# Four staging slots instead of two between the eviction and the store of relation products

## The reference

```
h = relu(layernorm(x))
# layer 0: a relational convolution, then a feed-forward part
xW  = einsum('nd,rde->nre', h, W_rel)        # 8 products per node
agg = segment_sum(xW[src, edge_type], dst)
y   = h + gelu(layernorm(agg + h @ W_self + b_conv))
x   = x + y + mlp(layernorm(y))
# layer 1: graph attention with 4 heads
xt = relu(layernorm(x)) @ W.T + bias
x  = x + segment_sum(xt[src] * softmax_over_dst(leaky_relu(...)), dst)
```

## Time and profile before

| | |
|---|---|
| median of three runs | 4581.68 us |
| profiled execution | 4576.85 us, its span 4575.1 us |
| busy share of PE, DVE, ACT, POOL | 55%, 55%, 13%, 70% |
| table stage: first store issued, last store issued | 21.77 us, 233.24 us |
| last store of the table stage landed | 235.86 us |
| stores of relation products | 98, of 512 KB each |
| gathers | 1680 from `rel_table`, 1664 from `xt_table` |

### The profile page before, as it was taken

How to read it: one execution, slowest core, us unless ns; L and a number is a source line. 1 busy time by engine, 2 the same in 40 slices (tenths; PEclk the granted TensorE clock), 3 DMA queues, 4 the chain that set the end, 5 groups by cost and what they waited for, 6 DMA issues and landing times.

```text
span 4575.1 us, 52415 instructions
## 1 busy us (share of the span) xinstructions
PE 2508.6 (55%) x13797; PEld 2111.2 (46%) x13902; DVE 2517.4 (55%) x6723; ACT 603.1 (13%) x1535; POOL 3194.7 (70%) x3372
## 2 busy tenths in 40 slices
PE   7923444444444444444433666666666666666664
PEld 3423343334434334443423556555555655555553
DVE  5652333333333333333334777777777777777777
ACT  4500111111111111111111000000000000000000
POOL 1077777777777777777746777777777777777772
PEclk9966676667667666766766777777777777877776
DMA  7722222222222222222213222222222222222222
GB/s 255 270 61 53 57 62 57 60 59 57 62 57 62 57 59 59 57 62 57 62 37 102 54 54 54 54 54 54 54 54 54 54 54 54 54 54 54 54 54 76
DMA packets 169389, 311.28 MB, mean 68 GB/s; under 512 B 58788, under 2 KB 99148, under 8 KB 168655
## 3 DMA queue, kind: packets, MB, share of 16 engines
q0 software_dynamic: 107008, 222.77, 20.2%
q1 hardware_dynamic: 46850, 81.19, 4.9%
q10 hardware_dynamic: 15490, 6.87, 0.6%
HBM read 239.51 MB, written 71.09 MB: 68 GB/s over the span
## 4 chain that ended last, share of the span: by engine, by line
POOL 66%; issue 23%; DVE 4%; DMA 3%; PE 2%; ACT 1%; POOLq 0%; DVEq 0%; ACTq 0%; SPq 0%
POOL G L490 66%; DMA rel_table<-G 2%; DMA G<-xt_table,idx 1%; DVE G L857 0%; DVE w L1223 0%; PE bank L1378 0%; PE bank L1379 0%; DVE G L1352 0%; DVE x_res L1354 0%; PE quad L1378 0%; PE quad L1379 0%; DVE edge L1226 0%; PE bank L1420 0%; ACT agg L724 0%; PE quad L1449 0%
## 5 line engine op out<-in xcount | busy, mean ns | idle before, releaser
L490 POOL DMA_INDIRECT G<-rel_table,idx x1680 | 1603.2, 954 | 743.6 <-issue 511.4
L490 POOL DMA_INDIRECT G<-xt_table,idx x1664 | 1570.7, 944 | 543.1 <-issue 502.3
L986 DVE SCALAR_TENSOR_TENSOR agg<-bank,sel,agg 128x128 f32 x208 | 64.2, 349 | 1057.0 <-PE bank L1420 1054.4
L1537 PEld LDWEIGHTS quad<-ident,top 128*128 128x128 f32 x3328 | 576.5, 272 | 143.8 <-issue 141.3
L1537 PE MATMUL quad<-ident,top 128*128 128x128 f32 x3328 | 585.1, 358 | 68.3 <-DVEq L1191 68.2
L1565 PE MATMUL bank<-M,onehot 128*128 128x132 f32 x3328 | 443.9, 289 | 172.5 <-DVE M L1240 172.5
L1565 PEld LDWEIGHTS bank<-M,onehot 128*128 128x128 f32 x3328 | 409.6, 198 | 204.5 <-issue 204.5
L1420 PE MATMUL bank<-G,onehot 128*128 128x128 f32 x1664 | 267.6, 336 | 391.2 <-DMA G<-rel_table,idx 386.8
L1420 PEld LDWEIGHTS bank<-G,onehot 128*128 128x128 f32 x1664 | 263.6, 253 | 395.8 <-issue 395.8
L1553 PE MATMUL bank<-Z,w_all 128*128 128x8 f32 x832 | 173.0, 337 | 442.7 <-issue 436.8
L1553 PEld LDWEIGHTS bank<-Z,w_all 128*128 128x128 f32 x832 | 166.2, 297 | 460.0 <-issue 459.8
(11 more groups left out here) (314 smaller groups left out, 3381.8 us busy)
## 6 DMA issues: line engine op xcount, KB each, us to landing
rel_table<-G SPq DMA_DIRECT2D x98, 512.0 KB, 2.7
G<-rel_table,idx POOLq DMA_INDIRECT x1680, 2.5
G<-xt_table,idx POOLq DMA_INDIRECT x1664, 2.7
xt_table<-w_all SPq DMA_DIRECT2D x25, 264.0 KB, 3.3
x_mid<-X SPq DMA_DIRECT2D x25, 256.0 KB, 2.0
out<-x_res SPq DMA_DIRECT2D x13, 448.0 KB
x_res<-in_x ACTq DMA_DIRECT2D x12, 448.0 KB, 4.4
x_res<-x_mid SPq DMA_DIRECT2D x3, 1792.0 KB, 10.5
```

Source lines behind the costliest of these rows:

```text
L490: g.indirect_dma_start(out=G[:, s, c, 0:width], out_offset=None, in_=table, in_offset=bass.IndirectOffsetOnAxis(ap=idx[:, s, c:c + 1], axi ...
L986: c.beside(v.scalar_tensor_tensor(row, banks[5 + k][:, 0:D], sel[:, w, bass.ds(g, 1)], row, ALU.mult, ALU.add))
L1537: ins = t.matmul(banks[j][:, hd * P:(hd + 1) * P], top[:, j, hd:hd + 1].to_broadcast([P, P]), ident[:, :], start=False, stop=(hd == HEADS ...
```

## The change

`STORES = 4` slots take the place of two. Block b uses slot b % 4, and each slot has its own semaphore `s_store[k]`, with a start value of 16 as before. ACT and DVE wait in block b for the store of block b-4. SP's loop runs 24 times over four blocks, and blocks 96 and 97 follow outside the loop; at the end SP waits for four semaphores. `hs`, `hT` and `typ_flat` move up by 2048 columns inside `G`. `hs`, `hT` and the two PSUM buffers of the products stay double.

```
+STORES = 4
+STORE_W = STORES * R * D
-        typ_flat = g_flat[0:GROUPS, 2 * R * D + 4 * D:2 * R * D + 4 * D + GROUP]
+        typ_flat = g_flat[0:GROUPS, STORE_W + 4 * D:STORE_W + 4 * D + GROUP]
-        xw = g_flat[:, 0:2 * R * D].rearrange("p (s n) -> p s n", s=2)
+        xw = g_flat[:, 0:STORE_W].rearrange("p (s n) -> p s n", s=STORES)
...
-        s_store = [sem("s_store0"), sem("s_store1")]
+        s_store = [sem(f"s_store{k}") for k in range(STORES)]
...
+            def store_block(b, k):
+                sp.wait_ge(xwA_sb, b + 3)
+                sp.wait_ge(xwB_sb, b + 3)
+                sp.dma_start(rel_table.rearrange("(n r) e -> n (r e)", r=R)[bass.ds(b * P, P), :],
+                             xw[:, k, :]).then_inc(s_store[k], 16)
+            with sp.Fori(0, BLOCKS // STORES) as i:
+                for k in range(STORES):
+                    store_block(i * STORES + k, k)
+            for b in range(BLOCKS // STORES * STORES, BLOCKS):
+                store_block(b, b % STORES)
+            for k in range(STORES):
+                sp.wait_ge(s_store[k], 16 * len(range(k, BLOCKS, STORES)) + 16)
...
-            def evict_high(b, j, pair):
+            def evict_high(b, j):
-                act.wait_ge(s_store[s], pair * 16 + 16)
-                a.copy(xw[:, s, 512:R * D], banks[2 + 3 * s][:, :]).then_inc(xwB_sb, 1)
+                act.wait_ge(s_store[b % STORES], b // STORES * 16 + 16)
+                a.copy(xw[:, b % STORES, 512:R * D], banks[2 + 3 * s][:, :]).then_inc(xwB_sb, 1)
...
-            def evict_low(b, s, pair):
+            def evict_low(b, s):
-                dve.wait_ge(s_store[s], pair * 16 + 16)
-                v.tensor_copy(xw[:, s, 0:512], banks[1 + 3 * s][:, :]).then_inc(xwA_sb, 1)
+                dve.wait_ge(s_store[b % STORES], b // STORES * 16 + 16)
+                v.tensor_copy(xw[:, b % STORES, 0:512], banks[1 + 3 * s][:, :]).then_inc(xwA_sb, 1)
```

More of the change, by code:

```diff
@@ L258, in build @@
         turn = s_flat[:, 5 * D + 24:5 * D + 24 + GROUPS].bitcast(i32)
-        xw = g_flat[:, 0:2 * R * D].rearrange("p (s n) -> p s n", s=2)
-        hs = g_flat[:, 2 * R * D:2 * R * D + 2 * D].rearrange("p (s n) -> p s n", s=2)
-        hT = g_flat[:, 2 * R * D + 2 * D:2 * R * D + 4 * D].rearrange("p (s n) -> p s n", s=2)
+        xw = g_flat[:, 0:STORE_W].rearrange("p (s n) -> p s n", s=STORES)
+        hs = g_flat[:, STORE_W:STORE_W + 2 * D].rearrange("p (s n) -> p s n", s=2)
+        hT = g_flat[:, STORE_W + 2 * D:STORE_W + 4 * D].rearrange("p (s n) -> p s n", s=2)
         hid = w_all[:, 0:2 * H].rearrange("p (s n) -> p s n", s=2)
@@ L394, in _ @@
                 sp.dma_start(tile[GROUPS - 1:GROUPS, 0:LAST], arr[full:E].rearrange("(g e) -> g e", g=1)).then_inc(s_edges, 16)
-            for k in range(2):
+            for k in range(STORES):
                 sp.sem_inc(s_store[k], 16)
[L398 to L406, removed]
+            def store_block(b, k):
[8 more added lines that the diff above has]
+                store_block(b, b % STORES)
+            for k in range(STORES):
+                sp.wait_ge(s_store[k], 16 * len(range(k, BLOCKS, STORES)) + 16)
             sp.sem_inc(tables_ready[0], 1)
@@ L617, in _ @@
                         act.wait_ge(h_norm, i + 2)
-                    evict_high(i * WIDE + j, j, i * (WIDE // 2) + j // 2)
+                    evict_high(i * WIDE + j, j)
                     load_ahead(i, j)
@@ L863, in low_round @@
                     more_stats(i, j)
-                evict_low(i * WIDE + j, j % 2, i * (WIDE // 2) + j // 2)
+                evict_low(i * WIDE + j, j % 2)
             turned(0, 0, [])
```

## The result

The changed kernel takes 4557.94 us (median of 5 runs, 4556.66 to 4560.1) against 4581.45 (4579.72 to 4583.63): ratio 0.995, 95% interval 0.9939 to 0.9962. In two later comparisons the gain at the medians was 22.5 and about 23 us. Between the first two profiled executions it is 19.3 us: 4575.1 to 4555.8 us of span.

A forecast was written before the change was run, and what follows sets the result against it. Waits for store slots were taken to bound the table stage, whose last store sets the kernel's end. Gains of rounds 0 to 6 summed to 16.85, say 17.0 us: 4581.68 - 17.0 = 4564.7 us, range 4559 to 4573.

The forecast's parts named there:

- The bound: Table stage, rounds 1 to 4: ACT and DVE wait for store slots; with four slots PE sets the pace.
- Loads of x: Table stage: two slots have 0.2 us of slack, and a load of x beside a store uses it up.
- Round by round, with round 5 as the measure of a round in which slots don't hold PE: Table stage: round 5's 26.15 us taken as PE's pace; rounds 2 and 3 fall to 26.2 us.
- rival B: Round 0: DVE gets its short steps in between two POOL instructions, 7.6 us more gain, 4557 us; chance 0.04.
- Round 1: Table stage: with weights W1, W2 and the linear weights besides, 30.80 to 27.2 us, gain 3.6.
- Round 0: Start of table stage: DVE still waits out POOL's block, block 6 copied at about 39.6; gain 0.7 us, bounds 0 and 2.5.
- The 84 rows: End of round 4: DVE waits 1.09 us for the last rows of x, PE's second buffer covers about half; 0.5 us stays.
- The change touches no gather: Behind the table stage: nothing in those 4340 us gets shorter; the kernel's end moves as much as the stage's last store.
- SP's two blocks outside the loop issue as in the loop: SP's blocks 96 and 97: no difference in issue; the new semaphores and increments cost under 0.1 us.
- A: Rival, table stage: DMA engines become the bound, not packed closer than 0.81; gain 8 us in all, 4574 us; chance 0.11.
- C: Rival, table stage: no change, stores wait behind each other whatever the slots; 4581.7 us; chance 0.06.
- D: Rival, round 0 onward: PE idles about 6.5 us and TensorE's low clock lasts; through round 1, 20 us slower, 4602; chance 0.03.

The follow-up runs named there:

- first experiment: Changed kernel with its four slots, but ACT and DVE wait for the store of block b-2 as before; 4577.84 us against 4578.69 for the kernel before.
- first try without loads of x: Kernel before, two slots, loads of x for rounds 3 to 6 left out and filled by POOL with a constant; 4571.53 us against 4578.69.

## Why the prediction was right or wrong

- **The bound** was right: the slot waits set rounds 1 to 4, they went, and PE took their place. Only the distance of the wait did it (first experiment).
- **Loads of x** as what uses up two slots' slack: right for 11.8 of 17.2 us, incomplete. Weight loads of 64 KB do it as well (rounds 1 and 2 of the first try without loads of x took 28.1 and 28.7 us), and with two slots a round without any other transfer still costs 0.8 us.
- **"Round by round, with round 5 as the measure of a round in which slots don't hold PE"** is the step that failed. A round that PE sets takes 25.8 us. The prediction had 14 x 1.83 = 25.6 for it, and read the 26.15 of round 5 as the same thing; but round 5 still held 0.8 us of slot cost around ACT's filling of `agg`: 2.27 and 2.38 us for two blocks, 1.83 and 2.01 in the changed kernel. Half of that was hidden, since the first seven blocks of the round took 12.5 us where the pace is 12.9: behind a stall the next blocks come faster. In the changed kernel the stall is the wait for the 84 rows; it shortens round 5 from 25.8 to 25.1 us, as the load moved earlier shows. With two slots it isn't shown that this wait is the reason: without other traffic rounds took 26.5 to 26.8 us, but in the first try without loads, which has no such wait, round 5 took 26.2 too.
- **The terms.** Term by term, forecast and measured gain, by the intervals between stores: round 1: 3.6, 5.0; round 2: 5.0, 5.4; round 3: 3.7, 4.1; round 4: 3.2, 2.6; round 5: 0.15, 1.1; round 6: 0.5, 1.1; round 0: 0.7, 0.8. With 0.3 us in the first store the sum is 20.4 at the last store, for 17. By the means of the three and four profiles the rounds 0 to 6 gained 1.1, 5.1, 4.8, 4.4, 2.6, 1.1 and 1.1 us. Round 6 was costed with 0.3 us for ACT's filling of `agg`, and four slots show none of it (2.17 us for that block, 2.14 for the others).
- **What that step explains.** The time is 6.8 us below the forecast's 4564.7. The rounds are 3.4 us of it. With 20.4 in the sum the forecast would have been 4561.3, inside the range; that the time fell below it comes with the 3.1 us by which the medians differ more than these last stores, see the last point. That it fell next to rival B's 4557 is chance, since B's way was not taken.
- **Round 1** at 27.2 for its weights: wrong by 1.4 us, the largest term. DMA share 0.99, PE without a gap. The estimate took a full DMA for a stall; with four slots, stores of that round took up to 5.2 us to land and nobody waited.
- **Round 0** was right by its mechanism. In the line numbers of before, I expected 776 to wait for line 466, 777 for 468 and 778 for the rest; in fact 777 got through as well, between 466 and 468, and 778 and 779 waited. The end, 39.6, is the same. The rule of the Trainium skill, page "SBUF — State Buffer", section "Who interferes with whom", agrees with this for the first two waits: 1.27 us behind line 474 and 4.37 behind 476 for 0.17 us of work, and 0.17 with POOL out of the way. The 3.11 us of the last step go further than the rule, which speaks of one instruction: they spanned four of POOL's, one close behind the other.
- **The 84 rows**: 1.65 us of wait instead of 1.09, and an interval of 3.3 us at the end of round 4 (before: the earlier trace rows):

```profile
159.06 0.68 DVE L780 BATCH_NORM_STATS2 stats<-x_res 128x6 f32<-128x128 f32 x3 [1.65 <-DMA x_res<-in_x]
```

  The prediction's half microsecond was too small; rounds 4 and 5 together show 52.4 - 51.6 = 0.8 us, and moving the load gave that back.
- **"The change touches no gather"** missed 1.0 us. "SP's two blocks outside the loop issue as in the loop" was wrong by 0.15 us; that moved POOL against DVE, and the order of two instructions turned.
- **Rivals.** A: the engines carried 0.99 where A allowed 0.81; by the loads made twice the bound begins just above. (A's own 4574 us also lay just outside the range that was said to hold most of it.) B: a gap of 0.08 us did let one more step through, but the last two still waited, and block 6 was copied at 39.59. C: not seen. D: PE idled 7.08 us and restarted at 40.53 in a window granted 0.50 (40.50 to 43.70), with 2.07 us for its first pair of records; but its pair of 44.13 took 1.02 us again, and from 45.10 to the end of round 0 the window stood at 1.00, as before.
- **What stays open.** At the last store the traces show 20.3 us, where the medians give 22.5 to 23.5. The two profiles of each kernel from one comparison come nearest: their spans are 22.2 us apart, the medians 22.7. Of the 22.2, 20.8 are there at the last store, 1.0 comes in the first 64 gathers, and 0.3 behind them. In the other two profiles of the changed kernel the stretch from the last gather of `rel_table` to the end took 2190.1 and 2191.0 us, and in these two, as in all three of before, 2187.8 to 2188.2. No run shows where these 2 to 3 us come from, or how often they come. The first profile of before was 4.6 us under its median, and I carried that over as equal for both; for the changed kernel it was 0.4 us above. How much of all this is chance isn't settled.

## What to carry to other kernels

Count a staging slot's time from the first copy into it to the landing of its store, and take the longest landing beside the other traffic, not the median of a quiet stretch. Here three slots, with 3 x 1.83 - 0.84 = 4.65 us for a landing, cover nearly all stores; two, with 2.8, fell short even in rounds without other traffic. For the floor of a round take the engine's own pace times the blocks, not the best round seen, which may live on credit from a stall before it. When a stall is removed ahead of a fixed one, look for what moves the fixed one: one raised wait on POOL was worth 8 us with four slots, and 5.7 with two.

## What the runs showed of the hardware

- DMA engines sustained 0.99 of their time, 352 GB/s, over the 25.8 us of round 1, in stores of 4 KB rows and loads of 512 byte rows together, and 362 GB/s with every load made twice.
- A store issued outside SP's loop went 0.72 us after its last copy had started, inside the loop 0.87 us. Those 0.15 us decided which of two instructions on DVE and POOL came first, and so 1.0 us of the first 64 gathers, in every profile of the two kernels.
- Steps of 0.17 us on DVE took 1.27 to 5.99 us beside POOL, and one of them lasted through four POOL instructions in a row.
